# A graph layer on one core: each group of matmuls in the edge loop signals through a drain behind it, not through its last matmul

## What is computed

```python
xn = layernorm(x)
# graph attention, 4 heads of 64
h = xn @ W
e = leaky_relu(a_src[src] + a_dst[dst], 0.2)        # an edge's score, self loops too
p = exp(e - segment_max(e, dst)[dst])
gnn = relu(segment_sum(p / segment_sum(p, dst)[dst] * h[src], dst) + bias)
# linear attention over all nodes, 8 heads of 32, then two dense layers with gelu
mix = gelu((q @ (ln(k).T @ ln(v)) / N + xn) @ w1 + b1) @ w2 + b2 + xn
x = x + gnn + mix
# mixture of 8 experts: the two best of a node by its logits
y = layernorm(x) * gamma + beta
w, top = softmax(top_2(y @ Wr + br))
x = x + sum(w[e] * (gelu(y @ W1[e] + b1[e]) @ W2[e] + b2[e]) for e in top)
```

## Time and profile before

| | us |
|---|---|
| timed, median of 3 runs | 2243.01 |
| timed, lowest and highest | 2241.64, 2247.39 |
| span of the profiled execution | 2629.1 |
| TensorE busy in it, matmuls | 1977.1 |
| VectorE, GpSimd, ScalarE busy | 1609.0, 1456.8, 1084.8 |

### The profile page before, as it was taken

How to read it: one execution, slowest core, us unless ns; L and a number is a source line. 1 busy time by engine, 2 the same in 40 slices (tenths; PEclk the granted TensorE clock), 3 DMA queues, 4 the chain that set the end, 5 groups by cost and what they waited for, 6 DMA issues and landing times. The chain is left out here.

```text
span 2629.1 us, 37526 instructions
## 1 busy us (share of the span) xinstructions
PE 1977.1 (75%) x9074; PEld 1396.6 (53%) x9075; DVE 1609.0 (61%) x3942; ACT 1084.8 (41%) x1932; POOL 1456.8 (55%) x1586
## 2 busy tenths in 40 slices
PE   8488887676766776766778777878888888898762
PEld 6365665554545554544555555555555666665431
DVE  7566666556666666586556665666765769553133
ACT  5322222234543443344545445555533655543110
POOL 3465656666666666655455555555565556530265
PEclk9788988887777777778888888898998998999876
DMA  9544544765555555545555555555556666531365
GB/s 319 142 133 132 141 123 116 221 185 143 160 153 144 156 151 148 151 129 148 147 167 158 149 153 142 150 149 146 146 152 165 163 166 160 155 109 59 116 194 168
DMA packets 286940, 401.66 MB, mean 153 GB/s; under 512 B 108852, under 2 KB 209492, under 8 KB 283199
## 3 DMA queue, kind: packets, MB, share of 16 engines
q0 software_dynamic: 74208, 206.08, 29.0%
q1 hardware_dynamic: 194348, 169.01, 21.9%
q10 hardware_dynamic: 18162, 24.08, 3.0%
HBM read 345.85 MB, written 81.96 MB: 163 GB/s over the span
## 5 line engine op out<-in xcount | busy, mean ns | idle before, releaser
L1534 POOL DMA_INDIRECT rows_g<-node_table,src_all x1347 | 1284.5, 954 | 922.1 <-issue 390.2
L2323 PE MATMUL psB<-rows_g,pick_e 128*128 128x260 f32 x2704 | 764.9, 441 | 111.7 <-issue 100.9
L2323 PEld LDWEIGHTS psB<-rows_g,pick_e 128*128 128x128 f32 x2704 | 589.6, 224 | 246.0 <-issue 141.7
L1709 DVE TENSOR_TENSOR rows_g<-rows_g,psD 128x2048 f32<-128x2048 f32 x169 | 384.9, 2277 | 0.0
L2122 ACT ACTIVATE pick_n<-local_row 128x1024 bf16<-128x1024 bf16 x169 | 178.6, 1057 | 389.6 <-remote 294.3
L1772 DVE COPY xn<-psD 128x256 f32<-128x256 f32 x112 | 47.4, 423 | 374.7 <-remote 143.7
L2364 PE MATMUL psC<-W_f,xnT 128*128 x448 | 246.3, 676 | 0.0
L2118 ACT ACTIVATE local_row<-local_row,minus_id 128x1024 bf16<-128x1024 bf16 x169 | 191.5, 1133 | 37.2 <-issue 25.2
L1680 DVE TENSOR_TENSOR pick_e<-psD,slot_all 128x1024 f32<-128x1024 f32 x169 | 203.8, 1206 | 0.1
L1556 POOL DMA_INDIRECT rows_g<-set_dram,places x98 | 96.2, 982 | 188.7 <-issue 165.3
L2312 PE MATMUL psA<-window,pick_n 128*128 128x24 bf16 x1352 | 61.2, 175 | 136.3 <-DVE psD L1690 49.8
(11 more groups left out here) (389 smaller groups left out, 3100.8 us busy)
## 6 DMA issues: line engine op xcount, KB each, us to landing
local_row<-local_dram SPq DMA_DIRECT2D x169, 256.0 KB
rows_g<-node_table,src_all POOLq DMA_INDIRECT x1347
xin<-sent_dram SPq DMA_DIRECT2D x112, 128.0 KB
set_dram<-xn SPq DMA_DIRECT2D x112, 128.0 KB
xnT<-in_xT_dram SPq DMA_DIRECT2D x96, 128.0 KB
sent_dram<-sorted_dram SPq DMA_DIRECT2D x96, 128.0 KB
sent_dram<-sorted_dram ACTq DMA_DIRECT2D x96, 128.0 KB
acc<-node_table SPq DMA_DIRECT2D x49, 128.0 KB
```

Source lines behind the costliest of these rows:

```text
L1534: pool.indirect_dma_start(out=rows_g[:, r, j], out_offset=None, in_=node_table, in_offset=bass.IndirectOffsetOnAxis(ap=src_all[:, g, j:j + ...
L1709: dve.tensor_tensor(heads, heads, p_here.unsqueeze(3).broadcast_to([P, EG, HEADS, C]), ALU.mult).then_inc(ph_ready, 1)
L2323: last = pe.matmul(ps_sum[s % 2][:, 0:AW], pick_e[:, s % SLOTS, j], rows_g[:, s % RING, j, 0:AW], start=(j == 0), stop=(j == EG - 1))
```

## The change

In every function of on_tensor that gives a signal, the increment is taken off the group's last matmul. Behind the group stands a drain instead, an instruction of TensorE's sequencer that carries the increment. Nothing else changes: the matmuls, their order, the waits, the other engines' lists and all DMAs are as before. One drain a group makes 1288 drains in the loop. The diff, cut to the pattern and its two variants; the other functions have the first form:

```diff
                     for j in range(EG):
-                        last = pe.matmul(ps_pick[:, j * 6 * HEADS:(j + 1) * 6 * HEADS], pick_n[:, j * P:(j + 1) * P],
+                        pe.matmul(ps_pick[:, j * 6 * HEADS:(j + 1) * 6 * HEADS], pick_n[:, j * P:(j + 1) * P],
                                          window[:, w].rearrange("p k a -> p (k a)"), start=True, stop=True)
-                    last.then_inc(picked, 1)
+                    pe.drain().then_inc(picked, 1)
...
                     for j in range(EG):
-                        last = pe.matmul(ps_sum[s % 2][:, 0:AW], pick_e[:, s % SLOTS, j], rows_g[:, s % RING, j, 0:AW],
+                        pe.matmul(ps_sum[s % 2][:, 0:AW], pick_e[:, s % SLOTS, j], rows_g[:, s % RING, j, 0:AW],
                                          start=(j == 0), stop=(j == EG - 1))
-                    last.then_inc(summed, 1)
+                    pe.drain().then_inc(summed, 1)
...
                     if t in SORTED:
                         pe.matmul(ps_small[:, count_at], after[:], both[:, i % 2], start=True, stop=True)
-                        pe.matmul(ps_small[:, total_at], ones_half[:], both[:, i % 2], start=True, stop=True).then_inc(counted, 1)
+                        pe.matmul(ps_small[:, total_at], ones_half[:], both[:, i % 2], start=True, stop=True)
+                        pe.drain().then_inc(counted, 1)
...
-                            kv_products(pe, pair_rows(e), 2 * (e % 2), len(pair_tiles(e)), e == PAIRS - 1).then_inc(kv_used, 1)
+                            kv_products(pe, pair_rows(e), 2 * (e % 2), len(pair_tiles(e)), e == PAIRS - 1)
+                            pe.drain().then_inc(kv_used, 1)
...
                         if s == PAIRS + 2:
                             pe.wait_ge(fold_dve, 1)
-                            spread_columns(pe, ps_hT).then_inc(fold_pe, 1)
+                            spread_columns(pe, ps_hT)
+                            pe.drain().then_inc(fold_pe, 1)
```

More of the change, by code:

```diff
@@ L2332, in turn_x @@
                     for c in range(KT):
-                        last = pe.transpose(ps_xT[:, c * P:(c + 1) * P], xe[:, u, c * P:(c + 1) * P], ident[:])
-                    last.then_inc(x_turned, 1)
+                        pe.transpose(ps_xT[:, c * P:(c + 1) * P], xe[:, u, c * P:(c + 1) * P], ident[:])
+                    pe.drain().then_inc(x_turned, 1)
                 experts = {}
@@ L2350, in up @@
                         for c in range(KT):
-                            last = pe.matmul(ps_up[0:rows, 0:D], xnT[:, u, c, 0:rows], weff[:, c], start=(c == 0), stop=(c == KT - 1))
+                            pe.matmul(ps_up[0:rows, 0:D], xnT[:, u, c, 0:rows], weff[:, c], start=(c == 0), stop=(c == KT - 1))
                     if kind == "block":
@@ L2363, in up @@
                         for c in range(KT):
-                            last = pe.matmul(ps_up[:, :], xnT[:, u, c], W1_f[:, bass.ds(e, 1), c], start=False, stop=(c == KT - 1))
-                    last.then_inc(up_done, 1)
+                            pe.matmul(ps_up[:, :], xnT[:, u, c], W1_f[:, bass.ds(e, 1), c], start=False, stop=(c == KT - 1))
+                    pe.drain().then_inc(up_done, 1)
                 def turn_h(n, kind, a, k):
@@ L2372, in turn_h @@
                     for c in range(parts):
-                        last = pe.transpose(ps_hT[:, c * P:c * P + rows], hid[0:rows, c * P:(c + 1) * P], ident[0:rows, 0:rows])
-                    last.then_inc(h_turned, 1)
+                        pe.transpose(ps_hT[:, c * P:c * P + rows], hid[0:rows, c * P:(c + 1) * P], ident[0:rows, 0:rows])
+                    pe.drain().then_inc(h_turned, 1)
                 def small_free(s):
@@ L2392, in down @@
                             pe.matmul(ps_small[0:rows, down_at], hidT[:, c, 0:rows], w2_s[:, c], start=(c == 0), stop=False)
-                        last = pe.matmul(ps_small[0:rows, down_at], ones_all[0:1, 0:rows], b2_row, start=False, stop=True)
+                        pe.matmul(ps_small[0:rows, down_at], ones_all[0:1, 0:rows], b2_row, start=False, stop=True)
                     if kind == "block":
@@ L2399, in down @@
                         for c in range(HK):
-                            last = pe.matmul(ps_small[:, down_at], turned_rows(n, kind)[:, c], W2_f[:, bass.ds(e, 1), c], start=False, stop=(c == HK - 1))
-                    last.then_inc(down_done, 1)
+                            pe.matmul(ps_small[:, down_at], turned_rows(n, kind)[:, c], W2_f[:, bass.ds(e, 1), c], start=False, stop=(c == HK - 1))
+                    pe.drain().then_inc(down_done, 1)
                 def turn_tile(t):
@@ L2408, in turn_tile @@
                     for k in range(KT):
-                        last = pe.transpose(ps_xT[:, (KT + k) * P:(KT + k) * P + rows], xd[0:rows, i % 3, k * P:(k + 1) * P], ident[0:rows, 0:rows])
-                    last.then_inc(x_turned, 1)
+                        pe.transpose(ps_xT[:, (KT + k) * P:(KT + k) * P + rows], xd[0:rows, i % 3, k * P:(k + 1) * P], ident[0:rows, 0:rows])
+                    pe.drain().then_inc(x_turned, 1)
                 def logits(t):
@@ L2415, in logits @@
                     for k in range(KT):
-                        last = pe.matmul(ps_small[0:rows, logits_at], xdT[:, k, 0:rows], wr_s[:, k], start=(k == 0), stop=(k == KT - 1))
-                    last.then_inc(logits_done, 1)
+                        pe.matmul(ps_small[0:rows, logits_at], xdT[:, k, 0:rows], wr_s[:, k], start=(k == 0), stop=(k == KT - 1))
+                    pe.drain().then_inc(logits_done, 1)
                 def count(t):
@@ L2428, in count @@
                     pe.matmul(ps_small[0:rows, count_at], after[0:rows, 0:rows], both[0:rows, i % 2], start=True, stop=False)
-                    pe.matmul(ps_small[0:rows, count_at], ones_half[:, 0:rows], seen_half[:], start=False, stop=True).then_inc(counted, 1)
+                    pe.matmul(ps_small[0:rows, count_at], ones_half[:, 0:rows], seen_half[:], start=False, stop=True)
+                    pe.drain().then_inc(counted, 1)
                 def sort(half, t):
@@ L2447, in kv @@
                     for k in range(KT):
-                        last = pe.matmul((ps_up, ps_hT)[u][0:rows, :], xnT[:, u, k, 0:rows], wkv_s[:, k], start=(k == 0), stop=(k == KT - 1))
-                    last.then_inc(kv_done, 1)
+                        pe.matmul((ps_up, ps_hT)[u][0:rows, :], xnT[:, u, k, 0:rows], wkv_s[:, k], start=(k == 0), stop=(k == KT - 1))
+                    pe.drain().then_inc(kv_done, 1)
                 def extra(kind, n):
@@ L2457, in extra @@
                         pe.wait_ge(row_ready, len(widths) + 1)
-                        last = pe.matmul(extra_cols(len(pieces)), ones_all[0:1], first_row, start=True, stop=True)
+                        pe.matmul(extra_cols(len(pieces)), ones_all[0:1], first_row, start=True, stop=True)
                     if kind == "piece":
@@ L2463, in extra @@
                         for j in range(PART):
-                            last = pe.matmul(extra_cols(cells_now), row_hot[n % 2][:, j], spot_hot[n % 2][:, j, 0:cells_now], start=(j == 0), stop=(j == PART - 1))
+                            pe.matmul(extra_cols(cells_now), row_hot[n % 2][:, j], spot_hot[n % 2][:, j, 0:cells_now], start=(j == 0), stop=(j == PART - 1))
                     if kind == "spread":
@@ L2467, in extra @@
                         for h in range(2):
-                            last = pe.matmul(extra_cols(2 * P)[:, h * P:(h + 1) * P], ones_all[:], ratio_diag[:, 2 * n + h], start=True, stop=True)
+                            pe.matmul(extra_cols(2 * P)[:, h * P:(h + 1) * P], ones_all[:], ratio_diag[:, 2 * n + h], start=True, stop=True)
                     if kind == "pair":
@@ L2473, in extra @@
                             for b in tiles:
-                                last = pe.matmul(extra_cols(AW)[:, h * C1:(h + 1) * C1], pair_weights[b % 4][:, h], node_rows_in[:, b % 6, h * C1:(h + 1) * C1],
+                                pe.matmul(extra_cols(AW)[:, h * C1:(h + 1) * C1], pair_weights[b % 4][:, h], node_rows_in[:, b % 6, h * C1:(h + 1) * C1],
                                                  start=(b == tiles[0]), stop=(b == tiles[-1]))
-                    last.then_inc(extra_done, 1)
+                    pe.drain().then_inc(extra_done, 1)
                 with pe.If(general_value(pe) == 0):
```

12 lines of the change are left out of this document (8 added, 4 removed).

## The result

The changed kernel takes 2678.51 us (median of 4 runs, 2674.76 to 2684.94), the kernel before in the same comparison 2244.82: a ratio of 1.1936, 95% interval 1.1913 to 1.1958, 434 us more. The forecast was 2620 with a range of 2470 to 2790.

A forecast was written before the change was run, and what follows sets the result against it. TensorE's own order was taken as the likeliest bound; from the timed 2243 us, about 530 us of drain costs less 168 us of idle cover gave 2605 at full cover, 2689 at half; forecast 2620, range 2470 to 2790.

The forecast's parts named there:

- The drain holds the sequencer: At TensorE's group ends: a drain keeps the sequencer until the matmuls are through, and 0.05 us more.
- The price on TensorE: Over the loop: 1012 group ends at 0.47 us, 476 us, plus 53 us of expert number loads, about 530 us.
- overlap: At a group's end: the next group's start under the group ahead is given up, 0.16 us.
- drain's end and restart: At a group's end: the drain's tail, 0.05 us, and from weight load to matmul, 0.11 us.
- the wait's part: Behind a drain: from a sequencer that wakes to the first weight load, 0.15 us; the uncertain term, at least 0.05.
- The value loads: On TensorE: 112 loads of an expert's number, 470 ns each, no longer hidden under matmuls, 53 us in all.
- The idle cover: In the loop: of TensorE's 554 us idle, 168 us are left in the timed runs to absorb the added time.
- the full price: At group ends: 0.47 us each; against it, a sequencer that writes no records may wake faster.
- rival of a better cover: In the loop: 0.37 us an end, all 554 us of idle time absorb most of it, 2300 to 2490; 14%.
- The clock: Over the loop: the granted clock falls with the gaps, 0.85 to 0.76, 218 us more, about 2840; 14%.
- The late signals: TensorE's late reports, as after the picks, are mostly the profiler's, some 436 us over a whole span.
- The idle price of 8 to 13 ns: At all 1288 drains: each costs what an idle one does, 10 to 17 us, time 2253 to 2260; 5%.

The follow-up runs named there:

- one more wait: An always met wait added behind each of the 1288 groups: on the kernel before 2244.28 us (ratio 0.9996), on the changed kernel 2789.83 us (1.2429).
- bare drain: Against the kernel before: signals stay on the last matmuls, and a drain without a signal stands behind each of the 1288 groups; 2689.39 us, ratio 1.1973.
- second profile: The kernel before, unchanged, run and profiled once more; 2245.25 us, ratio 1.000, profiled span 2246.3 us.
- moved loads: Changed kernel with 84 of 112 loads of an expert's number moved between the sums' matmuls and their drain; 2590.48 us, ratio 1.1544.
- first profile: The kernel before, unchanged, in the profile on which the prediction rests; span 2629.1 us, timed median 2243 us.
- second drain: Changed kernel with another drain, without a signal, behind each of the 1288 drains; 2856.71 us, ratio 1.2731.

## Why the prediction was right, and where it was by luck

**The drain holds the sequencer: right.** Drains last as long as the matmuls ahead, weight loads no longer start under the group ahead, and the one more wait, free without drains and paid with them, shows the reason. That the signal itself is no gain and no loss is shown by the bare drain.

**The price on TensorE: right in sum, 530 forecast, 549 measured.** The number of ends without a gap was 1012 by the earlier trace rows and is larger, since the second profile of before has fewer gaps: 1107 new short gaps and 112 with a value load, 1219. Their price is smaller: of the 264 + 113 = 377 us of gaps the loads are some 73 (0.65 us each: the 0.98 of a gap with a load less the 0.38 of one without, at 140.40, is 0.60, and the moved loads gave 0.68), so 304 + 172 = 476 us are left for 1219 ends, 0.39 us each where I took 0.47. By terms: overlap 0.14 (0.16 forecast), drain's end and restart 0.107 (0.05 + 0.11 forecast), the wait's part 0.122 (0.15 forecast). The 0.11 from weight load to matmul was read where the load ran under the group ahead; behind a drain it is 0.03 (146.04 to 146.07).

**The value loads: undersized.** 112 x 0.47 = 53 us counted what the load's instructions last; behind a drain each of them also has its distance to the next, and the gap grows by some 0.65, 73 us in the change, before the clock.

**The idle cover: wrong.** I had 168 us of idle time left in the timed runs, as 554 - 386, and the forecast stood near full cover, about 153. In the second profile TensorE is idle for 322 us of the loop (2013.00 - 1690.94); the longer gaps of the whole kernel hold 342 us, and 230 of them went: the 386 us of the first profile were not all idle time, 130 were TensorE's busy time (1977 against 1847). The step that failed is to take the difference of span and time wholly out of the idle time. What the prediction set against the full price, a sequencer that wakes faster without the recording, doesn't show: the changed kernel's recorded span, 2683.2 us, is within 0.2% of its timed median. And the rival of a better cover has a range that goes past its own condition: less than half of 427 us ends at 2456, not 2490.

**The clock: wrong to leave it out.** It was a rival of its own at 14%, on top of the forecast; it took 117 us within it. The sign that I named, a mean clock under 0.8, would have missed it: the mean is 0.871 after and 0.891 in the second profile of before, and the first profile of before, at about 0.844, made it look as if the clock had risen. My reason against it, that gaps under half a microsecond leave dense groups dense, is refuted by the sums at 140.40.

**The sum.** 549 - 230 + 117 = 436. The forecast had 530 - 153 + 0 = 377. Two misses, 77 us too little cover and 117 us of clock, nearly cancel; the range held the time for the right mechanism, but its middle owes something to that.

**The late signals: right for a wrong reason.** They aren't in the timed runs, as I took it, but they are not what a profile of this kernel always shows. The idle price of 8 to 13 ns fell with the second drain, which costs 0.077 us of gap although it lasts 13 ns.

## What to carry to other kernels

Where TensorE's sequencer ran ahead of its work here, waits, value loads and weight loads between groups were free; a drain, which holds it until the work is out, made each of them part of the path. So count all instructions that stand behind a drain, and not its own duration. No run here shows it for another engine. If a drain must be there, put it behind the next group's waits and value loads: that took half of this price away. And when a profile's span is far from the timed runs, take a second one before you build on its idle time or its clock.

## What was not expected of the hardware

With gaps of only 0.23 to 0.38 us between its groups, as from 136.63 to 140.40, TensorE's granted clock still falls to the lower level. Over the kernel it is there for 694 us instead of 493, and the 112 gaps of about 1 us at the value loads have a large part in that: with the loads of 84 of them moved it is 570. In the runs here each microsecond of gaps that was added behind drains (62 by one more wait, 112 by a second drain) came with 0.7 to 1.0 us lost to the clock (64 and 82). One more wait that is already met costs 0.12 us behind a drain, more than the 51 ns that it lasts.
